# The update gate's product in a recurrent kernel: scale from a tile in place of a column pointer

## The reference

```
def step(H, xs):
    xz, xr, xh = xs
    Z = jax.nn.sigmoid(xz + H @ Whz.T + bhz)
    R = jax.nn.sigmoid(xr + H @ Whr.T + bhr)
    H_tilda = jnp.tanh(xh + R * H @ Whh.T + bhh)
    H_new = Z * H + (1.0 - Z) * H_tilda
    Y = H_new @ Whq.T + bhq
    return (H_new, Y)
```

## Time and profile before

| | |
|---|---|
| median of 3 runs | 1236.14 us (1235.55 to 1236.6) |
| the profiled execution | 1237.86 us, span 1235.5 us |
| PE busy | 1219.9 us, 99% of the span |
| DVE busy | 892.1 us, 72% |
| ACT busy | 448.5 us, 36% |
| mean granted clock of TensorE | 0.994 |

### The profile page before, as it was taken

How to read it: one execution, slowest core, us unless ns; L and a number is a source line. 1 busy time by engine, 2 the same in 40 slices (tenths; PEclk the granted TensorE clock), 3 DMA queues, 4 the chain that set the end, 5 groups by cost and what they waited for, 6 DMA issues and landing times.

```text
span 1235.5 us, 54017 instructions
## 1 busy us (share of the span) xinstructions
PE 1219.9 (99%) x22459; PEld 1175.9 (95%) x22480; DVE 892.1 (72%) x5771; ACT 448.5 (36%) x2252; POOL 65.5 (5%) x50
## 2 busy tenths in 40 slices
PE   7999999999999999999999999999999999999998
PEld 6899999999999999999999999999999999999865
DVE  3467777777777777777777777777777777777665
ACT  1233333333333333333333333333333333333332
POOL 2300000000000000000000000000000000000000
PEclk7999999999999999999999999999999999999999
DMA  9401010011111000001001111101111100111000
GB/s 350 179 21 28 29 28 12 19 29 29 29 29 29 4 28 29 29 29 29 13 19 29 29 29 29 29 5 27 29 28 29 29 10 22 29 29 24 7 7 7
DMA packets 42885, 43.84 MB, mean 35 GB/s; under 512 B 7416, under 2 KB 39424, under 8 KB 41360
## 3 DMA queue, kind: packets, MB, share of 16 engines
q1 hardware_dynamic: 40288, 38.91, 10.8%
q10 hardware_dynamic: 2128, 0.89, 0.3%
q0 software_dynamic: 224, 0.59, 0.2%
HBM read 35.70 MB, written 4.69 MB: 33 GB/s over the span
## 4 chain that ended last, share of the span: by engine, by line
PE 98%; DMA 1%; DVE 1%; ACTq 0%; issue 0%; ACT 0%; DVEq 0%
PE bank L367 54%; PE gate_rh L367 32%; PE gate_z L367 12%; DMA rbias<-in_rbias 1%; DVE rhp L1033 0%; ACT rg L749 0%; DVE osb L976 0%; ACTq L812 0%; ACTq L814 0%; ACTq L811 0%; ACTq L813 0%; ACTq L810 0%; DVE x L968 0%; ACTq L809 0%; DVE x L957 0%
## 5 line engine op out<-in xcount | busy, mean ns | idle before, releaser
L749 ACT ACTIVATE rg<-gate_rh 128x16 f32<-128x16 f32 x512 | 94.4, 184 | 458.3 <-PE gate_rh L367 458.3
L367 PEld LDWEIGHTS gate_rh<-state,whp 128*128 128x128 f16 x6144 | 233.4, 96 | 22.0 <-DVE state L1049 10.2
L367 PE MATMUL gate_rh<-state,whp 128*128 128x8 f16 x6144 | 249.6, 167 | 0.6 <-DVE state L1049 0.6
L367 PEld LDWEIGHTS gate_rh<-rhp,whp 128*128 128x128 f16 x6144 | 228.9, 96 | 14.9 <-DVE rhp L1033 9.7
L367 PE MATMUL gate_rh<-rhp,whp 128*128 128x8 f16 x6144 | 237.2, 167 | 1.5 <-DVE rhp L1033 1.4
L1033 DVE SCALAR_TENSOR_TENSOR rhp<-rg,hist 128x16 f16<-128x16 f32 x512 | 89.6, 175 | 162.6 <-ACT rg L749 153.9
L367 PE MATMUL gate_z<-state,whp 128*128 128x16 f16 x4096 | 179.9, 176 | 0.0
L749 ACT ACTIVATE zg<-zsum 128x16 f32<-128x16 f32 x512 | 110.5, 216 | 167.4 <-DVE zsum L1038 167.4
L367 PE MATMUL bank<-xt,rw 128*128 128x128 f32 x1024 | 166.7, 293 | 0.0
L367 PE MATMUL bank<-ge,rw 128*128 128x128 f32 x1024 | 164.2, 289 | 0.0
L1043 DVE TENSOR_SCALAR zin<-zg,nsscale 128x16 f32<-128x16 f32 x512 | 120.4, 235 | 56.1 <-ACT zg L749 38.7
(11 more groups left out here) (159 smaller groups left out, 1611.2 us busy)
## 6 DMA issues: line engine op xcount, KB each, us to landing
gates<-gates_t SPq DMA_DIRECT2D x30, 512.0 KB, 5.4
aw<-in_aw SPq DMA_DIRECT2D x4, 2048.0 KB, 23.8
out<-osb SPq DMA_DIRECT2D x32, 128.0 KB, 4.3
xt<-in_xT SPq DMA_DIRECT2D x30, 128.0 KB, 5.4
rw<-in_rw SPq DMA_DIRECT2D x2, 1024.0 KB, 11.1
sw<-in_sw SPq DMA_DIRECT2D x3, 512.0 KB, 6.9
wh<-in_wh SPq DMA_DIRECT2D x3, 256.0 KB, 13.7
wx<-in_wx SPq DMA_DIRECT2D x3, 256.0 KB, 20.7
```

The costliest lines, as they stand in the source:

```text
L367: return pe.matmul(o, w, x, start=start, stop=stop, skip_group_check=True)
L749: return act.activation(o, i, f, **kw)
```

## The change

`nsscale` grows from a column (one number per partition) to a tile of 128 x 2 x 8 elements, which is the state's shape. The operation at L1043 becomes a scalar_tensor_tensor with two tiles as inputs, in place of a tensor_scalar with one tile and a column that is read through a pointer. In the preamble the tile is set to -1 and then multiplied by the scale in place, still through a pointer. Nothing changes place; no wait is added or removed; PE, ACT, POOL and SP have the same instructions as before.

```
-        nsscale = sb("nsscale", [P, 1])
+        nsscale = sb("nsscale", [P, KC, B])
...
                     dve.wait_ge(zg_done, n)
-                    dve.tensor_scalar(zin[:, :, :, 1], zg[:], -1.0, nsscale[:], ALU.add, ALU.mult)
+                    dve.scalar_tensor_tensor(zin[:, :, :, 1], zg[:], -1.0, nsscale[:], ALU.add, ALU.mult)
                     dve.wait_ge(half_done, n)
...
             dve.memset(hin[:], 0.0)
+            dve.memset(nsscale[:], -1.0)
             dve.wait_ge(cond_in, 32)
...
             dve.memset(seed[:, 3], 0.0).then_inc(biases, 1)
-            dve.tensor_scalar(nsscale[:], sscale[:], -1.0, None, ALU.mult)
+            dve.tensor_scalar(nsscale[:], nsscale[:], sscale[:], None, ALU.mult)
             dve.wait_ge(peaks_dve, 11)
```

## The result

| | before | after |
|---|---|---|
| median of 6 runs | 1235.88 us | 1231.38 us |
| span of the profiled execution | 1235.5 us | 1229.1 us |
| DVE busy | 892.1 us | 867.2 us |

The ratio is 0.996, with a 95% interval of 0.9948 to 0.9972: 3.5 to 6.4 us faster, 4.5 by the medians. The forecast was 1231.8 us, 4.3 us faster.

What follows compares the result with a forecast made beforehand. Long steps were taken as bound by PE, short ones by the circle of state, reset gate, candidate, scan and low part. 214 short steps x 0.02 us, preamble at nothing: 1236.14 - 4.3 = 1231.8 us, range 1230.5 to 1235.2.

Steps and rivals of the forecast that it cites:

- Two kinds of steps, and only the short ones count: Steps behind six filler records (short, 214 of 512) are bound by the state's circle; those behind eight (long) by PE.
- the stand: PE waiting about 0.09 us inside the state's matmul group in short steps, before the ninth matmul, for the low part.
- The pointer is what L1043 pays for: At L1043 the column pointer costs about 70 ns: 235 ns would become 169, and L1045 start 0.06 us sooner.
- Only a part of it is gained: At the scan, 0.02 us of the 0.06 is gained; the other 0.04 turns into waiting for ACT's half of hin.
- 214 x 0.02 = 4.3 us: Total gain: short steps times the scan's earlier start, between 4 and 5 us with rounding of the distances.
- The preamble at nothing: Added memset and wider nsscale write lie in DVE waits and cost nothing; uncovered, together 0.12 us.
- DVE's busy time: Over 512 steps DVE's busy time falls by 512 x 66 ns = 34 us.
- The rule on two-tensor operations: By the skill's table alone, L1043's new form is some 8 ns longer, the kernel about 1.7 us slower.
- Rival 1: The scan starts 0.05 us after ACT's half whatever DVE does: no gain, 1236.1 us (1234 to 1236.2); chance 0.10.
- rival 2: Another link in the short steps' circle, or PE's filler, takes up the gain: about 1236 us; chance 0.07.
- rival 3: At L1043 the second tile is streamed as extra work and the pointer's cost stays: 1239.7 us; chance 0.05.
- Rival 4: ACT's way is shorter or more steps stand: 0.025 per step, 5.3 us, 1230.8 us; 0.78 together with the forecast.

Runs made afterwards that it cites:

- tile_short: Changed kernel with the new tile form of L1043 only in steps 10 to 15 of each block, the pointer form elsewhere: 1230.88 us, ratio 0.9954.
- tile_long: Changed kernel with the new tile form of L1043 only in steps 0 to 9 of each block, the pointer form elsewhere: 1235.62 us, ratio 0.9997.
- gap14: Changed kernel with fourteen small memsets on a spare tile between L1043 and L1045, delaying L1045: 1258.27 us, ratio 1.0186.
- imm: Changed kernel with L1043 as a one-tile tensor_scalar with constant -2048.0 as scale, no pointer or second tile (state not the reference's): 1230.11 us, ratio 0.9948.
- stt_ptr: Changed kernel with L1043 as a two-tile scalar_tensor_tensor that also reads a column through a pointer: 1237.87 us, ratio 1.0014.
- gap3: Changed kernel with three small memsets on a spare tile between L1043 and L1045: 1230.25 us, ratio 0.9961.
- preamble: Kernel before with only the preamble's half of the change; L1043 stays a tensor_scalar reading the tile's first column through a pointer: 1235.84 us, ratio 1.0006.
- gap6: Changed kernel with six small memsets on a spare tile between L1043 and L1045: 1234.62 us, ratio 0.9993.
- waits_after: Changed kernel with the scan's two waits exchanged, DVE's zh_done first and ACT's ht_done second: 1245.99 us, ratio 1.009.
- waits_before: Kernel before, with the pointer, with the scan's two waits exchanged, zh_done first and ht_done second: 1245.67 us, ratio 1.0079.

## Why the prediction was right, point by point

- *Two kinds of steps, and only the short ones count.* Shown by `tile_short` and `tile_long`, and from the other side by `gap14`. The count of 214 stood (211 in the profile after). One reading on the way there was wrong: the 602.59 of the earlier trace rows isn't where the state's group starts, only where the record in front of it has ended, and with 0.19 us for eight matmuls it would leave no stand at all. The group starts at 602.43, by PE's timeline of the kernel before:

```profile
602.43 0.54 PE L367 MATMUL gate_rh<-state,whp 128*128 128x8 f16 x12
```

  With 0.19 us behind 602.43 the ninth matmul is due at 602.62, ahead of the low part at 602.66, so the stand is there and the conclusion holds.
- *The pointer is what L1043 pays for.* Shown by `imm` and `stt_ptr`: about 60 ns of record with either form, where the prediction had about 70. The forecast length was 169 ns and it is 176, which no run explains; L1045's start came 0.051 us sooner, the low end of the bounds of 0.05 to 0.07.
- *Only a part of it is gained.* The forecast was that 0.02 of 0.06 is gained and the rest turns into waiting for ACT. Measured, by the medians of short steps: of 0.051, 0.022 are gained (the scan stands 0.032 behind ACT where it stood 0.054) and 0.029 are room (0.132 behind DVE's half where it stood 0.103); DVE's half can be delayed by 0.025 (`gap3`) without a loss. The extra idle time ahead of the scan is there, 68.6 us against 54.1 in the kernel before:

```profile
L1049 DVE TENSOR_TENSOR_SCAN state<-zin,hin 128x32 f16<-128x32 f32 x512 | 115.2, 225 | 54.1 <-ACT hin L749 0.9 <-DVE hin L1045 0.9
```

  But the profile puts only 2.3 of it down to ACT, not most of it as I had said; it names no cause for gaps as short as these (0.13 us each).
- *The size.* The term "214 x 0.02 = 4.3 us" was right within what can be told: the medians say 4.5, with an interval of 3.5 to 6.4. Its bounds were not: "between 4 and 5" has 0.05 less 0.03, but 0.06 less 0.03 would be 6.4 us. Between the two profiles a short round fell by 0.028, not 0.022. In 211 steps that is 5.9 us, which is also what the stretch from the first scan to the last fell by (1161.7 to 1155.8); the other 0.5 of the 6.4 that the span fell lies ahead of the first scan, which comes at anything from 67.3 to 69.1 us in the traces of this case. But a part of the 0.028 belongs to the one profiled execution of the kernel before, and not to the change. Its long rounds (steps 2 to 8) took 2.317, where those of all other traces took 2.313 to 2.315; and in `preamble`, with the same operations and distances in the step, a short round took 2.182 and not 2.187. Against `preamble` the short round fell by 0.023, which is 4.9 us in 211 steps.
- *The preamble at nothing.* Shown by its own run, to within 0.2%.
- *DVE's busy time* fell by 24.9 us, not 34. Busy time counts overlapping records once, so it falls by the distance (512 x 0.051 = 26), which the prediction had used everywhere but there.
- *The rule on two-tensor operations* (the Trainium skill, VectorE: DVE Perf Modes, "The perf-mode tier table") gives 8 ns for the second tile as an estimate. In the distance it is 0.009 between `imm` and the changed kernel (the records are 176 ns in both), so the distance agrees with it; what decided was the pointer, of which that table says nothing.

Rival 1 fell with the scan's 0.03, rival 2 with the rounds, rival 3 with L1043's 176 ns. Rival 4, a gain of 0.025 per step, can't be told from the forecast: the rounds say 0.023 to 0.028, and the interval of the medians holds both.

Does a short round follow the scan's distance from ACT and nothing else? Nearly: `gap6` against `gap3` has the scan 0.024 later and the round 0.026 longer, `stt_ptr` against the changed kernel 0.033 and 0.032, `waits_after` 0.069 and 0.069. What stays open is why the profiled execution of the kernel before was slower than `preamble` by 0.005 us a short round and 0.003 a long one. The granted clock was 1.00 in both from 100 us to 1200 us, so it isn't that.

## What to carry to other kernels

Before an operation on a busy loop is made cheaper, ask which of the waits behind it binds: the one whose distance to the waiter is the same in all steps, which need not be the one whose record ends last. The gain is then the smaller of what the operation saves and the room to the next binder, times the steps in which the loop and not the filler sets the pace. And where one instruction has two waits, write first the one whose event comes last; here the wrong order cost 10 to 15 us, more than twice what the change gained.

## What the runs showed of the hardware

- Reading a column through a pointer made a 128x16 float32 operation on DVE about 60 ns longer (176 to 236 ns) and its follower 0.05 to 0.06 us later, in a tensor_scalar (`imm` against the kernel before) and in a scalar_tensor_tensor (the changed kernel against `stt_ptr`) alike.
- Of two semaphore waits ahead of one DVE instruction the one written last cost 0.10 us from the end of the awaited operation's record to the start of the instruction, for an event of DVE (the kernel before) and of ACT (`waits_after`, `waits_before`); the one written first cost 0.03 for an event of ACT (the changed kernel).
- A memset of one column of 128 partitions took 59 ns of record but only 0.008 us from start to start, up to the seventh in a row; there followed one step of 0.05 (`gap14`).
